# Two streams of batch rows side by side, in four stages in place of five

## The reference

```
x = LN(x + sparse_attention(x))     # per query: 64 local keys + 32 picked by index scores; 8 heads, latents of 32
x = LN(x + 16_experts(x))           # sigmoid router, best 4 of 16, silu(gate)*up, plus one shared expert
x = LN(x + selective_scan(x))       # in_proj, conv of 4, silu, delta, 16 states: state = exp(delta*A)*state + delta*B*u
x = LN(x + top1_experts(x))         # 8 experts, capacity 256 tokens over all 4 rows in order (a running count)
```

## Time and profile before

| | us |
|---|---|
| median of three runs | 1391.71 |
| span of the profiled execution | 1397.1 |
| DVE busy in it | 1001.4 (72%) |
| PE busy in it | 899.8 (64%) |
| ACT busy in it | 557.8 (40%) |
| POOL busy in it | 84.1 (6%) |
| mean granted clock of PE | 0.774 of full |

### The profile page before, as it was taken

The page is one execution under the profiler, slowest core; times in us unless marked ns, Lnnn a source line. Parts: engine busy times, 40 slices in busy tenths (PEclk is TensorE's granted clock), DMA queues, the critical chain, the costliest instruction groups (busy, mean ns, idle before and its releaser), DMA issues.

```text
span 1397.1 us, 29245 instructions
## 1 busy us (share of the span) xinstructions
PE 899.8 (64%) x11808; PEld 542.2 (39%) x11808; DVE 1001.4 (72%) x2303; ACT 557.8 (40%) x1250; POOL 84.1 (6%) x56
## 2 busy tenths in 40 slices
PE   4655757687656678687747567687747667471455
PEld 2534535454333245354424235354423335240122
DVE  5455553666689987665689987765779997654985
ACT  3232232465643332465553232366554232355310
POOL 0000000011000000011000000011000000030630
PEclk8556758788769779587758989698758879786896
DMA  4110110211223310121123210031033310112420
GB/s 144 32 39 10 33 40 11 64 39 38 68 65 85 77 31 11 39 70 39 40 73 94 76 42 6 14 92 39 10 93 91 80 50 4 43 34 62 118 63 8
DMA packets 85079, 72.20 MB, mean 52 GB/s; under 512 B 24784, under 2 KB 63696, under 8 KB 84752
## 3 DMA queue, kind: packets, MB, share of 16 engines
q1 hardware_dynamic: 84944, 70.34, 19.3%
HBM read 66.51 MB, written 3.80 MB: 50 GB/s over the span
## 4 chain that ended last, share of the span: by engine, by line
DVE 38%; PE 30%; ACT 13%; issue 13%; DMA 3%; SPq 2%; DVEq 0%; POOL 0%; ACTq 0%; POOLq 0%
PE bank L723 6%; DVE SG L1749 5%; PE bank L550 4%; PE bank L755 2%; DVE Y L1842 2%; ACT relu_s L1034 2%; PE bank L881 2%; DVE XP L1762 2%; DVE CV L1762 2%; SPq L486 2%; PE bank L831 2%; DVE ml L1477 2%; DVE bank L1749 1%; DVE big L1737 1%; PE bank L832 1%
## 5 line engine op out<-in xcount | busy, mean ns | idle before, releaser
L723 PE MATMUL bank<-onehot,tparts 128*32 128x256 bf16 x3840 | 137.0, 304 | 51.2 <-DVE onehot L1523 51.2
L723 PEld LDWEIGHTS bank<-onehot,tparts 128*32 128x32 bf16 x3840 | 110.7, 107 | 87.0 <-issue 75.0
L881 PE MATMUL bank<-XP,CO 128*128 128x512 f32 x128 | 84.2, 792 | 63.2 <-DVE XP L1760 34.4
L1749 DVE TENSOR_TENSOR_SCAN SG<-big 128x512 f32<-128x512 f32 x96 | 111.7, 1204 | 0.9
L1224 ACT ACTIVATE big<-DEL,Aneg 128x512 f32<-128x512 f32 x96 | 63.8, 714 | 102.7 <-DVE SG L1749 96.7
L1034 ACT ACTIVATE relu_s<-bank,nml 128x192 f32<-128x192 f32 (+1 forms) x128 | 52.8, 424 | 111.6 <-DVE nml L1482 111.6
L881 PE MATMUL bank<-CV,CO 128*128 128x512 f32 x128 | 74.3, 710 | 33.5 <-DVE CV L1762 21.2
L1477 DVE TENSOR_REDUCE ml<-bank 128x2 f32<-128x384 f32 (+1 forms) x64 | 33.7, 568 | 68.8 <-PE bank L658 37.6
L1523 DVE TENSOR_SCALAR onehot<-ib,CO 128x1024 bf16<-128x1024 f16 x160 | 69.9, 480 | 14.2 <-PE bank L723 12.8
L755 PE MATMUL bank<-GT,QBD 128*32 128x32 f32 x3072 | 57.2, 209 | 34.6 <-DVE G L1532 23.6
L550 PE MATMUL bank<-CO,relu_s 128*128 128x128 f32 (+2 forms) x256 | 46.6, 343 | 47.6 <-ACT relu_s L1034 47.6
(11 more groups left out here) (309 smaller groups left out, 1992.4 us busy)
## 6 DMA issues: line engine op xcount, KB each, us to landing
BC<-bc_rows SPq DMA_DIRECT2D x128, 256.0 KB, 4.4
ib<-idx_rows SPq DMA_DIRECT2D x64, 256.0 KB, 4.1
rows_bounce<-RO SPq DMA_DIRECT2D x256, 8.5 KB
big<-comb_rows SPq DMA_DIRECT2D x16, 256.0 KB, 4.5
big<-comb_rows SPq DMA_DIRECT2D x8, 512.0 KB, 8.5
W<-w SPq DMA_DIRECT2D x1, 2818.0 KB, 14.3
RB<-rows_bounce SPq DMA_DIRECT2D x16, 136.0 KB, 2.1
X<-x SPq DMA_DIRECT2D x4, 256.0 KB, 2.8
```

The source lines that it names most:

```text
L723: m = mm(bank[2 + c % 2][32 * bb:32 * bb + 32, 256 * kind:256 * kind + 256], tparts[:, kt, part, 32 * kind:32 * kind + 32], onehot[:, n % ...
L881: mm(bank[5 + j][:, :], ident, hC[(n - 1) % 2][:, j, :], start=(n == 1), stop=(n == DS)).then_inc(ysum.sem, ysum.up())
L1749: m = dve.tensor_tensor_scan(state, decay, dBu[:, n % 2, j, :], 0.0, ALU.mult, ALU.add)
```

## The change

The loop over rows is written anew as two streams, which each engine takes alternately, one phase of each per step, **the second stream first**:

- first stream: keys and attention of row 0, attention 2, attention 3, rest 2
- second stream: 7 idle steps (`LAG`), keys and attention of row 1, rest 0, rest 1, rest 3

So the pairs are attention 0 with 1, attention 2 with rest 0, attention 3 with rest 1, rest 2 with rest 3. An attention with its keys has 64 phases (later ones 60, since their keys stand in the end of the one before), a rest 62. Counted in steps: attention 1 ends at 71, rest 0 stands at 71 to 133, rest 1 at 133 to 195, rest 3 at 195 to 257; attention 2 at 64 to 124, attention 3 at 124 to 184, rest 2 at 184 to 246.

- There are two sets of attention tiles and two sets of rest tiles (set 1 of the one lies where set 0 of the other does), each with four PSUM banks. `onehot`, `QBD` and `GT` exist once and serve both attentions: the four one-hot slots go round over both, and a stream that spreads its queries or writes picked keys waits for the picked scores that stand before it in PE's order (`picks_before`).
- With four banks, the local output shares a bank with the local scores: its first half now waits until ACT has taken both groups' exponentials (`pl_ok`), ACT copies the finished local output to SBUF (`ol_sb`), and the merge of the tile before moves from phase 4 to phases 5 and 6.
- `alone`, `TWICE` and `close` are gone; every rest runs in the form that stood beside an attention. The norm ahead of the rest is its first phase. The experts' gate and up take turns in three banks, so that the next gate product need not wait for the product of the one before; the last layer's outputs take turns in four banks.
- ACT spreads the queries for all tiles of rows 0 and 1; DVE for tiles 0 and 1 of rows 2 and 3.
- The semaphores count over the whole program, and the rows of B and C share one semaphore per slot.

The core of the diff:

```diff
-        def weave(first, second):
-            step = 0
-            live = [first, second]
-            while live:
-                for g in list(live):
-                    for _ in range(2 if g is second and step in TWICE else 1):
-                        if g in live and next(g, "end") == "end":
-                            live.remove(g)
-                step += 1
...
-            weave(keys(0), iter(()))
-            weave(attention(0), iter(()))
-            close(0)
-            for b in range(1, B - 1):
-                weave(attention(b), rest(b - 1))
-                close(b)
-            weave(attention(B - 1, last=True), rest(B - 2))
-            close(B - 1)
-            weave(rest(B - 1, alone=True), iter(()))
+        following, preceding = {0: 2, 2: 3}, {2: 0, 3: 2}
...
+        def streams(first_keys, keys, tiles, merges, rest, begun=0):
...
+            def first():
+                yield from idle(begun)
+                yield from first_keys
+                yield from attention(0)
+                yield from attention(2)
+                yield from attention(3)
+                yield from rest(2)
+
+            def second():
+                yield from idle(LAG)
+                yield from keys(1)
+                yield from attention(1)
+                yield from rest(0)
+                yield from rest(1)
+                yield from rest(3)
+
+            for _ in both(second(), first()):
+                pass
 
         def spread_by_dve(b, i):
 
-            return i < 2 or b == 0
+            return b >= 2 and i < 2
+
+        def picks_before(b, i):
+
+            return sr_ps.before(b, i + 1)
+
+        def slot_of(b, n):
+
+            return (oh_ok.at(b, n + 1) - 1) % 4
+
+        def gate_bank(k):
+
+            return (0, 1, 3)[2 * k % 3]
...
+        attentions = (first_attention, second_attention, first_attention, first_attention)
+        rests = (first_rest, first_rest, second_rest, first_rest)
...
                     def local_out(g):
                         pe.wait_ge(pt_sb.sem, pt_sb.at(b, 2 * i + g + 1))
                         if g == 0:
-                            free = at_used if i >= 1 else attn_done
-                            pe.wait_ge(free.sem, free.at(b, i))
+                            pe.wait_ge(pl_ok.sem, pl_ok.at(b, 2 * i + 2))
...
+                    act.wait_ge(ol_ps.sem, ol_ps.at(b, 2 * i + 2))
+                    A(own.On[:, 0, :, :].rearrange("p h c -> p (h c)"), own.bank[2][:, 256:512], ACT.Copy).then_inc(ol_sb.sem, ol_sb.up(b))
...
-                    if k >= T:
-                        pe.wait_ge(ga_used.sem, ga_used.at(b, k - T + 1))
+                    if k >= 2:
+                        pe.wait_ge(ga_used.sem, ga_used.at(b, k - 1))
+                    mm(own.bank[gate_bank(k)][0:rows, :], wg, own.XRT[:, :], start=True, stop=True).then_inc(ga_ps.sem, ga_ps.up(b))
+                    if k >= 1:
+                        pe.wait_ge(gx_ok.sem, gx_ok.at(b, k))
+                    mm(own.bank[up_bank(k)][0:rows, :], wu, own.XRT[:, :], start=True, stop=True).then_inc(up_ps.sem, up_ps.up(b))
```

More of the change, by code:

```diff
@@ L399, in both, with idle @@
+        def idle(steps):
+            for _ in range(steps):
+                yield
         def both(first, second):
@@ L495, in merges, with rest @@
                     yield
-            def rest(b, alone=False):
-                sp.wait_ge(rest_done.sem, rest_done.at(b, 0))
+            def rest(b):
+                own = rests[b]
+                sp.wait_ge(*space_free(b))
                 for _ in range(ROUTE_PHASES):
@@ L983, in keys @@
-                softplus_logs(b, act_k, kr, [kr_e[:, s, :, :] for s in range(3)], kr_sp)
+                kr = own.bank[0][:, 0:256].rearrange("p (n c) -> p n c", n=NT)[:, :, 32:64]
+                softplus_logs(b, act_s, kr, [own.kr_e[:, s, :, :] for s in range(3)], kr_sp)
                 yield
@@ L1286, in merges, with rest @@
                     yield
-            def close(b):
-                pass
-            def rest(b, alone=False):
-                pool.wait_ge(rest_done.sem, rest_done.at(b, 0))
+            def rest(b):
+                own = rests[b]
+                pool.wait_ge(*space_free(b))
                 for _ in range(ROUTE_PHASES + 2):
@@ L1644, in rest @@
+                dve.wait_ge(vec.sem, vec.now(b))
+                dve.reciprocal(own.rs[:, 1, :], own.rs[:, 0, :]).then_inc(vec.sem, vec.up(b))
+                dve.wait_ge(vec.sem, vec.now(b))
+                STT(out=own.rt[:, 5, :, :], in0=own.rt[:, 4, :, :], scalar=ROUTE,
+                         in1=own.rs[:, 1, :].unsqueeze(2).to_broadcast([P, NT, NE]), op0=ALU.mult, op1=ALU.mult).then_inc(comb_ok.sem, comb_ok.up(b))
                 dve.wait_ge(comb_ok.sem, comb_ok.now(b))
                 yield
-                T, lag = turns(alone), 1 + alone
@@ new lines, in vector_program @@
+            dve.wait_ge(set_v.sem, set_v.now("setup"))
+            dve.transpose(rank_turn[:, :, :], first_attention.SR[:, 0:2, :]).then_inc(set_v.sem, set_v.up("setup"))
+            dve.wait_ge(set_v.sem, set_v.now("setup"))
+            assert set_v.rows["setup"] == SET_VEC
+            streams(keys(0), keys, tiles, merges, rest)
+        programs = (sync_program, tensor_program, scalar_program, gpsimd_program, vector_program)
+        for program in programs:
+            program(Count())
```

1654 lines of the change are left out of this document (832 added, 822 removed).

## The result

The changed kernel takes **1414.34 us** (median of four runs, 1408.4 to 1416.76), the kernel before in the same job 1392.26 us; the ratio is 1.0154, with a 95% interval of 1.0128 to 1.0181. It is slower by 22 us, where the prediction had 1306 and a range up to 1365.

A forecast was written before the change was run, and what follows sets the result against it. No engine bounds the whole; lone stages are one chain of latencies that a second stream would fill. 45 + 326 + 578 + 318 + 44 = 1311 us, so 1306 against the median; 8-in-10 range 1245 to 1365.

The forecast's parts named there:

- Sum 457.8, and over 1.46 that is 314: Attention 0 with 1: PE and DVE work at today's paired rate takes 314 us; 326 taken with new waits.
- little overlap of equals: Rival: like streams overlap only halfway, attentions at 1.30 (352 us), rests at 1.32 (337 us); kernel 1351 us; chance 15%.
- The query spread leaves DVE ... 24 more of 839 ns go to ACT: Attention pair: 16 fewer DVE copies in each of the two rows, 8.8 us each, leaving DVE 224.6 us.
- PE 2 x 116.6 = 233.2: Attention pair: PE busy 233.2 us, each attention costing what it does beside another stream, clock near 0.80.
- The new waits of PE: Attention pair: local output waits for ACT's second exponentials, at most 4.8 us per attention exposed; ACT's output copy costed at nothing.
- a large new wait of DVE for one-hot slots: Attention pair: named, with one of PE for exponentials, as a sign that the prediction was wrong; no size given.
- The middle, 578: Attentions 2 and 3 with rests 0 and 1: work of 844 over 1.46 takes 578 us, allowed 555 to 620.
- The rest pair, 318: Rest 2 with rest 3, steps 184 to 246: work of 445.2 over 1.46 is 305 us, taken as 318.
- A rest has 123.0 of DVE: DVE work of one rest: paired stage's 244.1 us less attention's 121.1; used for the middle and rest pair.
- POOL beside DVE: Rest pair: at most 5 us by rows, costed at nothing; by the skill's port rule some 22 us, kernel 1328.
- Start and tail: Steps 0 to 7, 45 us as now; last 11 phases of rest 3 alone, 44 us.
- The signs of being wrong: First-stretch clock near 0.65, a large PE wait for exponentials or DVE wait for one-hot slots, or middle over 40 us late.

The follow-up runs named there:

- e14: Changed kernel with the query spread of rows 0 and 1 on DVE in all tiles instead of ACT: 1395.16 us, ratio 1.0022, attention pair 357.5 us.
- b1: Kernel before with only the new wait added, PE waiting for both halves of the local probabilities in all tiles: 1392.05 us, ratio 1.0001.
- e2: Changed kernel with the attention ahead of the rest in steps 71 to 183 alone: 1411.49 us, ratio 1.0151.
- e6: Changed kernel with the picks of rows 0 and 1 using one of the three bf16 parts of the table: 1400.56 us, ratio 1.0066.

## Why the prediction was wrong

- **"Sum 457.8, and over 1.46 that is 314"** (the attention pair): this step failed, and with it half of the error. The rate 1.46 was measured on an attention beside a rest and put on two attentions. They made 1.24, against 1.14 alone; e14, the shortest pair, made 1.33, with 18 us of copies now counted on DVE. The rival "little overlap of equals" named this and mis-sized it: it had 1.30 and 352 us. The reason given against it, that today's pairs meet the same waits, did not carry over: the present pairs are an attention with a rest. For its other half, two rests, the rival was wrong: they made 1.43. Why two attentions overlap less is shown in part: 21 of the 53 us are the ACT copies of the next point. That the long DVE operations of a rest fit into an attention's waits, and another attention's short ones don't, is my reading, and no run tests it.
- **"The query spread leaves DVE ... 24 more of 839 ns go to ACT"**: I counted 8.8 us saved on DVE and nothing on ACT, by its busy share. e14 undoes it: 19 us of the 22 that the change lost. ACT's busy share was as read, and said nothing about its queue. At a lag of 6 the sign is the other, so this is a price at this place and not one of ACT as such.
- **"PE 2 x 116.6 = 233.2"**: it was 251.7. The clock did rise, 0.65 to 0.76 and not to 0.80, and `L730` took 402 ns, even less than the 443 of the earlier trace rows. The picks hold most of the 18.5: 42 us in each attention for the 34.7 beside a rest, 15 us in all.
- **The new waits of PE**, costed at nothing: right for this one. The wait for exponentials ended 9.6 us of PE's idle time, and b1 shows no cost. What I named as "a large new wait of DVE for one-hot slots" is 14.7 us in the pair (`DVE onehot <- PE bank`), against 8.6 in one attention alone; the large one is PE's for one-hots.
- **The middle, 578**: it took 617. 33 us more of work than the 844, at 1.46 22 us, and a rate of 1.42, 16 us. Of the 33, 18 are PE's (412.1 for 394), whose clock was 0.76 and 0.78 there and not 0.79 and 0.80, and 15 are DVE's. By the earlier trace rows a rate of 1.44 was the lowest seen, and the two stages that this middle replaces had 1.46 and 1.48. In every changed kernel run here it is 1.40 to 1.44. The order in a step (e2) and the wait for exponentials (b1) do not explain it; the shared banks were not tested, and the place of the scan against the attention was moved by a step or two only, so this loss stays open.
- **The rest pair, 318**: it took 329, at 1.43 nearly the rate, with 26 us more work, all of it DVE's (272.3 for 246.0). "A rest has 123.0 of DVE" was too small: 244.1 is the least of three stages, whose mean is 248.0, and the 121.1 taken off it are row 0's, with 16 query copies where the others have 8. By the means a rest has 248.0 - 116.7 = 131.3, which gives 17 of the 26. DVE is busy for 83% of the stretch; whether it bounds it was not tested.
- **POOL beside DVE**, costed at nothing: 9 us of DVE's time, 5 of them in the middle; the rows follow.
- Start and tail: right to 2 us.
- **The signs of being wrong**: none came. The clock was 0.76, neither of the two named waits was large, and the middle was 39 us longer than 578, where I had named 40. No sign asked for the pair's rate, the one number that failed.

In 1041.2 to 1370 us, where 16 POOL products fall, DVE's products of the earlier trace rows's kind are these groups:

```profile
L1726 DVE TENSOR_TENSOR HT<-SG,U 128x512 f32<-128x512 f32 x10 | 7.9, 793 | 13.0 <-ACT SG L1249 8.1 <-POOL U L1374 4.8
...
L1726 DVE TENSOR_TENSOR HT<-SG,SZ 128x512 f32<-128x512 f32 x6 | 4.1, 690 | 2.8 <-ACT SG L1249 1.4 <-POOL U L1374 1.3
```

The 793 is a mean of nine products of 0.69 us and one of 1.69, which started while POOL was at a product:

```profile
1113.97 1.26 POOL L1374 TENSOR_TENSOR SZ<-SZ,big 128x512 f32<-128x512 f32 x1
1114.10 1.69 DVE L1726 TENSOR_TENSOR HT<-SG,U 128x512 f32<-128x512 f32 x1 [0.85 <-ACT SG L1249]
```

The 1012 of the earlier trace rows is likewise a mean, of 683, 684 and 1669 ns, so the prediction's 0.33 us per product was really 1 us for one of three. In the changed kernel nine DVE instructions that met a POOL product took 0.95 to 1.08 us longer than their likes, 9.0 us in all: four in the rest pair, and in the middle four one-hots (1.50 us for 0.48) and a small one. The rule of the Trainium skill, page "SBUF — State Buffer", section "SBUF: two separate sides", is that the loser of the shared port blocks for the whole instruction; the section limits it to DVE instructions in a 2-port mode, or with two SBUF inputs while GpSimd reads SBUF. These delays go its way, each somewhat shorter than POOL's product (1.26 to 1.45 us). The scans that the prediction held against it read one input from PSUM (`bank<-bank,big`), so the section does not speak of them. What was wrong in the 22 us is the count: of 16 products in the rest pair, four met such an instruction.

What stays open: why the spread on DVE changes its sign between a lag of 7 and of 6, some 30 us between the best pair seen (357) and the 326 predicted, and the middle's lower rate. More one-hot slots might free DVE from PE's picks; it wasn't tried.

## What to carry to other kernels

A rate of overlap belongs to the pair on which it was measured: here it was 1.47 for attention with rest, 1.43 for two rests and 1.24 for two attentions, and the first was 1.42 in the new order. Compare stretches before and after by work and length together, since a new order also moves work between them. The cost of a move to an idle engine depends on what stands behind it in that engine's queue. Where streams meet at a fixed offset, the offset is worth a series of runs: between 7 and 6 steps it moved the kernel by 32 us, more than the change.

## What the runs showed of the hardware

- 96 pick matmuls took 2.80 us at a granted clock of 1.00, where PE had been busy for 4.2 of the 4.7 us before, and 4.41 and 4.47 at 0.61, which is a mean of the levels of 1.2 and 2.4 GHz, right after PE had been idle for 3.5 and 1.8 us.
- With 1,280 matmuls fewer (e6), the granted clock in the pair went from 0.76 to 0.64 and each `L730` from 402 to 487 ns; half of the 46 us came back in the other matmuls.
- A copy of 32x768 took 552 ns on DVE and 838 on ACT.
- A DVE instruction that met a POOL product took about 1.0 us longer in nine cases of the changed kernel.
- The same order of instructions, run in two jobs, agreed to 0.6 us in the median, but to 4 us in one stretch of the profile.
